# First two node tiles of the first linear share its weight rows, with matmuls on a tile of ones at the start

## What is computed

```
def sage(h, W_self, W_neigh, b):
    mean = segment_sum(h[src], dst) * deg_inv
    return h @ W_self + mean @ W_neigh + b
h   = relu(sage(x, W_self0, W_neigh0, b0))
x   = layernorm(x + sage(h, W_self1, W_neigh1, b1))
g   = x @ W.T + b                          # self loops added to the edges
out = layernorm(x + segment_sum(norm * g[col], row))
```

## Time and profile before

| | |
|---|---|
| median of 3 runs | 884.67 us (883.26 to 888.33) |
| span of the profiled execution | 879.3 us |
| time of that execution around its span | not given; the median lies 5.4 us above the span |
| mean granted TensorE clock | 0.995 |
| busy: TensorE, its weight loads, VectorE, ScalarE, GpSimd | 857.7, 731.8, 383.8, 142.9, 414.3 us |
| HBM | 114.83 MB read, 69.69 MB written |

### The profile page before, as it was taken

One profiled execution on the slowest core, in us unless ns is written; L12 is line 12 of the kernel. 1 busy time (PEld: TensorE's weight loads), 2 busy tenths in 40 slices (PEclk: granted clock), 3 DMA queues, 4 the chain that ended last, 5 costly groups with the idle time before them and its releaser, 6 DMA issues.

```text
span 879.3 us, 11251 instructions
## 1 busy us (share of the span) xinstructions
PE 857.7 (98%) x4403; PEld 731.8 (83%) x4403; DVE 383.8 (44%) x684; ACT 142.9 (16%) x199; POOL 414.3 (47%) x343
## 2 busy tenths in 40 slices
PE   6999999999899999999999999999999999999996
PEld 5888888888898899788888888888889889988885
DVE  5365669000037757411134112236664634555554
ACT  4111131202112113200031000011111212200000
POOL 2318878877878868877768857820000000000000
PEclk9999999999989999999999999999999999999999
DMA  8999665554777896433395788875648657755551
GB/s 305 312 425 349 213 195 144 142 153 110 183 234 214 263 291 197 116 100 98 102 360 175 241 269 286 249 221 165 215 132 291 206 167 249 252 187 196 194 192 47
DMA packets 111994, 185.56 MB, mean 211 GB/s; under 512 B 16526, under 2 KB 87190, under 8 KB 105792
## 3 DMA queue, kind: packets, MB, share of 16 engines
q1 hardware_dynamic: 60496, 113.56, 39.3%
q10 hardware_dynamic: 39056, 56.26, 18.1%
q0 software_dynamic: 12384, 14.95, 7.3%
HBM read 114.83 MB, written 69.69 MB: 210 GB/s over the span
## 4 chain that ended last, share of the span: by engine, by line
PE 90%; DVE 3%; DMA 3%; ACT 2%; issue 1%; ACTq 1%; SPq 0%; DVEq 0%
PE ps L1164 47%; PE ps L1192 11%; PE ps L1243 10%; PE ps L1257 10%; PE ps L1223 7%; DMA xin<-s0t_scr 2%; PE ps L1148 1%; PE ps L1106 1%; ACT outb L648 1%; PE ps L1116 1%; PE ps L1212 1%; DMA xin<-in_x 0%; ACT w L606 0%; DMA raw<-in_L_gnn_W_neigh 0%; DVE sacc L1039 0%
## 5 line engine op out<-in xcount | busy, mean ns | idle before, releaser
L1164 PE MATMUL ps<-w,xs 128*128 128x512 f32 x1440 | 335.0, 393 | 3.1 <-ACT w L606 1.8
L1164 PEld LDWEIGHTS ps<-w,xs 128*128 128x128 f32 x1440 | 270.2, 189 | 60.3 <-ACT w L606 3.0
L541 POOL DMA_INDIRECT adj_in<-mult,idx_in x160 | 199.9, 1250 | 82.2 <-issue 82.2
L541 POOL DMA_INDIRECT adj_out<-loops,idx_out x160 | 198.8, 1242 | 70.4 <-issue 66.0
L1192 PE MATMUL ps<-xs,w 128*128 128x512 f32 (+1 forms) x576 | 109.4, 351 | 1.2 <-ACT outb L648 1.1
L1192 PEld LDWEIGHTS ps<-xs,w 128*128 128x128 f32 x576 | 93.9, 189 | 16.8 <-ACT outb L648 1.8
L1164 PE MATMUL ps<-u,xs 128*128 128x512 f32 x432 | 98.2, 389 | 0.0
L1223 PE MATMUL ps<-w,u 128*128 128x256 f32 (+5 forms) x640 | 96.1, 312 | 0.0
L1164 PEld LDWEIGHTS ps<-u,xs 128*128 128x128 f32 x432 | 81.0, 188 | 16.8
L1223 PEld LDWEIGHTS ps<-w,u 128*128 128x128 f32 (+1 forms) x640 | 88.2, 194 | 6.6
L1243 PE MATMUL ps<-u,xs 128*128 128x512 f32 (+1 forms) x400 | 91.3, 390 | 0.3 <-issue 0.3
(11 more groups left out here) (135 smaller groups left out, 601.8 us busy)
## 6 DMA issues: line engine op xcount, KB each, us to landing
xs<-xt_scr SPq DMA_DIRECT2D x30, 1024.0 KB
xt_scr<-xs ACTq DMA_DIRECT2D x10, 1024.0 KB, 8.3
xin<-in_x SPq DMA_DIRECT2D x18, 512.0 KB, 7.4
xs<-xt_scr SPq DMA_DIRECT2D x16, 512.0 KB, 3.9
adj_in<-u POOLq DMA_DIRECT2D x4, 1600.0 KB, 26.1
adj_out<-u POOLq DMA_DIRECT2D x4, 1600.0 KB, 46.4
w<-adj_in SPq DMA_DIRECT2D x5, 1280.0 KB, 8.6
xs<-adj_in SPq DMA_DIRECT2D x10, 640.0 KB, 5.4
```

What stands on the lines that cost most here:

```text
L541: pool.indirect_dma_start(table, bass.IndirectOffsetOnAxis(ap=index[0:EP, j:j + 1], axis=0), counts[0:EP, j:j + 1], None, bounds_check=CEL ...
L1164: ins = nc.tensor.matmul(acc[:, cols], xs[:, t % 2, k, left * T:(left + 1) * T], w_row(q, k, right)[:, cols], start=(i == 0), stop=(i == l ...
```

## The change

It does five things.

- SyncE loads node tile 1 right after weight row 0.
- TensorE first runs 30 matmuls of 128 columns of a tile of ones with itself, into bank 7, as soon as VectorE's early memsets are done (`WARM_UP`).
- A new function `first_two` takes the place of `linear(N0, 0)` and `linear(N0, 1)`. For rows 0 to 4 (`SHARED = 5`) it does the steps of both tiles with a row before it goes to the next one; then tile 0 does rows 5 to 7 alone, and then tile 1. Tile 1 is turned right after the first pair of matmuls, into banks 6 and 7 (`turn_pair`), tile 2 between tile 0's last step and tile 1's own rows.
- ScalarE rounds tile 1 right after row 0's high part, stores turned tile 0 after row 5 and turned tile 1 after row 7. VectorE makes tile 1's low part right after row 0's.
- b0's transposition moves behind tile 1.

```diff
+    SHARED, WARM_UP = 5, 30
...
+        def turn_pair(t):
+            return 3 if t == 1 else 2
...
             load_x(0)
-            for k in range(4):
-                load_w(N0, k)
+            load_w(N0, 0)
             load_x(1)
-            for k in range(4, KD):
-                sp.wait_ge(w_lo_done, k - 3)
+            for k in range(1, KD):
+                if k >= 4:
+                    sp.wait_ge(w_lo_done, k - 3)
                 load_w(N0, k)
...
             for k in range(KD):
                 split_hi(N0, k)
-            store_turned(0)
-            for t in range(NT):
+                if k == 0:
+                    turn_hi(1)
+                elif k in (5, 7):
+                    store_turned(k // 2 - 2)
+            evict_hi(N0, 0)
+            for t in range(1, NT):
...
             for k in range(KD):
                 split_lo(N0, k)
+                if k == 0:
+                    turn_lo(1)
...
-                if t >= 1:
+                if t >= 2:
                     pe.wait_ge(xt_lo_done, t)
...
+            def first_two():
+                shared = []
+                for k in range(SHARED):
+                    for t in range(2):
+                        shared += [(t, k, 0, 0), (t, k, 1, 0)]
+                    if k >= 1:
+                        shared += [(0, k - 1, 0, 1), (1, k - 1, 0, 1)]
+                own = [[(t, SHARED - 1, 0, 1)] + [(t, k, left, right) for k in range(SHARED, KD) for left, right in ((0, 0), (1, 0), (0, 1))]
+                       for t in range(2)]
+                for i, (t, k, left, right) in enumerate(shared + own[0] + own[1]):
+                    if i == 1:
+                        turn_tile(1)
+                    elif i == len(shared) + len(own[0]):
+                        turn_tile(2)
+                    if k == 0:
+                        pe.wait_ge(xt_lo_done if left else xt_hi_done, t + 1)
+                    if t == 0 and left == 0:
+                        pe.wait_ge(w_lo_done if right else w_hi_done, k + 1)
...
+            pe.wait_ge(ones_ready, 3)
+            for _ in range(WARM_UP):
+                nc.tensor.matmul(ps[:, 7, 0:P], ones_r[:, :], ones_r[:, :], start=True, stop=True)
             pe.wait_ge(ident_ready, 1)
             turn_tile(0)
-            for t in range(NT):
-                linear(N0, t)
+            first_two()
+            for t in range(1, NT):
+                if t > 1:
+                    linear(N0, t)
```

More of the change, by code:

```diff
@@ L577, in turn_hi @@
                 act.wait_ge(xt_turned, t + 1)
+                if t == 1:
+                    act.wait_ge(xt_hi_done, 1)
                 if t >= 2:
                     act.wait_ge(xt_stored[t % 2], 16 * (t // 2))
-                nc.scalar.activation(xs[:, t % 2, :, 0:T], by_tile(pair_bank(2)), ACT.Copy).then_inc(xt_hi_done, 1)
+                nc.scalar.activation(xs[:, t % 2, :, 0:T], by_tile(pair_bank(turn_pair(t))), ACT.Copy).then_inc(xt_hi_done, 1)
             def store_turned(t):
@@ L772, in turn_lo @@
                 dve.wait_ge(xt_hi_done, t + 1)
-                nc.vector.tensor_tensor(xs[:, t % 2, :, T:2 * T], by_tile(pair_bank(2)), xs[:, t % 2, :, 0:T].bitcast(F32), ALU.subtract
+                nc.vector.tensor_tensor(xs[:, t % 2, :, T:2 * T], by_tile(pair_bank(turn_pair(t))), xs[:, t % 2, :, 0:T].bitcast(F32), ALU.subtract
                                         ).then_inc(xt_lo_done, 1)
@@ L906, in _ @@
                 if t + 1 < NT:
-                    turn_lo(t + 1)
+                    if t >= 1:
+                        turn_lo(t + 1)
                     if t == 1:
@@ L1102, in turn_tile @@
                 pe.wait_ge(x_full[t % 2], 16 * (t // 2 + 1))
-                if t >= 1:
+                if t >= 2:
                     pe.wait_ge(xt_lo_done, t)
                 for k in range(KD):
-                    ins = nc.tensor.transpose(ps[:, 4 + k // 4, k % 4 * T:(k % 4 + 1) * T], xin[:, t % 2, k * P:(k + 1) * P], ident[:, :])
+                    ins = nc.tensor.transpose(pair_bank(turn_pair(t))[:, k * T:(k + 1) * T], xin[:, t % 2, k * P:(k + 1) * P], ident[:, :])
                 ins.then_inc(xt_turned, 1)
@@ L1141, in linear @@
                 steps = sum((high[k] + (low[k - lag] if k >= lag else []) for k in range(KD)), []) + sum(low[KD - lag:], [])
-                if q == N0 and t == 0:
-                    steps[1:3] = steps[2:0:-1]
                 if q == GCN and t == NT - 1:
@@ L1152, in linear @@
                 for i, (k, left, right) in enumerate(steps):
-                    if q == N0 and t < NT - 1 and i == (16 if t == 0 else 4):
+                    if q == N0 and t < NT - 1 and i == 4:
                         turn_tile(t + 1)
@@ L1169, in linear @@
                         ins.then_inc(w_used, 1)
+            def first_two():
[16 more added lines that the diff above has]
+                        pe.wait_ge(w_lo_done if right else w_hi_done, k + 1)
+                    for n in range(2):
+                        cols = slice(n * BANK, (n + 1) * BANK)
+                        ins = nc.tensor.matmul(pair_bank(acc_pair(N0, t))[:, cols], xs[:, t, k, left * T:(left + 1) * T], w_row(N0, k, right)[:, cols],
+                                               start=(k + left + right == 0), stop=(k == KD - 1 and right == 1))
+                    if k == KD - 1 and right == 1:
+                        ins.then_inc(acc_full, 1)
             def self_turned():
@@ L1289, in _ @@
                     general = pe.value_load(flag[0:1, 0:1], min_val=0, max_val=1)
-                if t == 0:
-                    pe.wait_ge(ones_ready, 3)
+                if t == 1:
                     pe.wait_ge(b0_full, 16)
```

## The result

The changed kernel took 891.49 us (median of 6 runs, 888.39 to 894.06), the kernel before beside it 885.98 us (6 runs, 883.26 to 888.33): ratio 1.0067, 95% interval 1.0045 to 1.009. That is 5.5 us slower, outside the forecast range, which ended at 887.0 us.

A forecast was written before the change was run, and what follows sets the result against it. TensorE, busy 98% of the 879.3 us span, was taken as the bound; tile 1 ending 2.0 us early, less 1.2 us of new wait for the flag step, gained 0.8 us: 883.9 us, range 881.0 to 887.0.

The forecast's parts named there:

- the clock that was to be up before the linear: TensorE's clock was to rise at 6.3 to 7.1 us, so the first linear would start at the high level.
- the way of the edge lists to VectorE: Edge loads were to be released 1.35 us later with the same times to landing, the flag step done at 43.03 us.
- the mis-sized warm-up: 30 TensorE matmuls at 0.11 us each, done at 4.7 us, ahead of tile 0's landing at 5.19, costing nothing.
- the upper of my bounds: At most 0.213 us per 128-column warm-up matmul, with two passes; the warm-up would then end at 7.8 us.
- The 226-column row: Nearest profiled matmul form, 18 in 2.17 us, read as no more than one pass; used to take 0.11 us.
- rival 3: Warm-up on TensorE is in the way: tile 0 turned 1.4 us later, 885.3 us in total; chance 0.11.
- Rival 1: TensorE's clock doesn't come up before the linear: 885.0 us, or 886.1 if gaps delay the rise; chance 0.23.
- 2.2 us of slack: At TensorE's one-column flag-summing matmul in tile 2: VectorE's flag step ended at 41.68 us, the matmul ran at 43.89.
- my sum (33.7 + 8.14): Tile 1's end plus the way to the flag matmul: TensorE there at 41.85 us, waiting until about 43.05; 0.8 us gained.
- Later than 22.6 us the kernel is slower: Break-even for the end of row 7's high split on ScalarE, which gates the edge loads; forecast at 21.8 us.
- the absence of gaps behind the last of tile 1's row-0 pairs: From 12.25 us TensorE was to starve for nothing in the first linear, so tile 1 ends at 33.7 us.
- Rival 3's large case: Each short warm-up matmul costs as much as a 512-column one, 0.427 us: everything behind 7.9 us late, 891.7 us; chance 0.04.

The follow-up runs named there:

- e4: Changed kernel with 7 warm-up matmuls of 512 columns instead of 30 of 128; ratio 1.0035 to the kernel before.
- e2: Changed kernel with 14 warm-up matmuls of 128 columns instead of 30; ratio 1.0027 to the kernel before.
- e3: Kernel before with the 30 warm-up matmuls of 128 columns as its only change; ratio 1.0027 to the kernel before.
- e9: Changed kernel run once more, unaltered; ratio 1.0058 to the kernel before.
- e6: Changed kernel with 7 warm-up matmuls of 512 columns and edge loads issued behind row 4's high split instead of row 7's; ratio 0.9991 to the kernel before.
- e8: Kernel before with 7 warm-up matmuls of 512 columns and edge loads issued behind row 4's high split instead of row 7's; ratio 0.9993.
- e10: Changed kernel with 7 512-column warm-ups, edge loads behind row 4's high split, zero fills held until the edge lists landed; ratio 1.0031 to the kernel before.
- e14: Changed kernel with 7 warm-up matmuls of 512 columns and the flag matmul moved from tile 2 to tile 3; ratio 1.0007 to the kernel before.
- e1: Changed kernel without the warm-up matmuls, all else of the change kept; ratio 1.0052 to the kernel before.
- e16: Changed kernel without warm-up, stores of turned tiles 0 and 1 moved later on ScalarE; ratio 1.0023 to the kernel before.
- e11: Changed kernel without warm-up, zero fills held until the edge lists landed; ratio 1.006 to the kernel before.
- e13: Changed kernel without warm-up, flag matmul moved from tile 2 to tile 3; ratio 1.003 to the kernel before.

## Why the prediction was wrong

Two steps failed: the clock that was to be up before the linear, and the way of the edge lists to VectorE, which was to stay as long as it was. The first, with the mis-sized warm-up, made TensorE late; the second made the kernel slower even where the clock was up (e4).

- **Warm-up, mis-sized.** I took 0.11 us for a 128-column matmul of float32r; it took 0.213 from start to start, the upper of my bounds. The 226-column row that I let decide was of matmuls at the high clock, where a second pass or a fixed cost can't be read off a comparison with 512 columns at the low one. The first pair came 2.6 us later; rival 3 had 1.4 us for this, since it kept the transposes fast.
- **The clock, the first step that failed.** I had it up at 6.3 to 7.1 us. No narrow warm-up (changed, e2, e3, e9) raised it ahead of the linear; 7 wide matmuls, 3.36 us in all (e4, e6, e8, e10, e14), raised it before the linear's first pair in each profile. What part the transposes between play isn't separated by any run. Rival 1 happened, on top of rival 3. I had priced them apart, never together: with both, tile 1's rounding ends at 15.2 us instead of 10.96.
- **The way of the lists, the second step that failed.** I saw that row 7's high split gates the edge loads and that the flag matmul had 2.2 us of slack. I moved the gate by 1.35 us; it moved 5.7 in the changed kernel, 3.1 in e1 (24.30 against 21.16; rival 1 had 2.5) and 1.2 in e4, where the clock was up. From issue to key step I kept 17.3 us; it took 18.5 in the changed kernel, 19.3 in e1 and 20.5 in e4. So even with the forecast clock the flag matmul goes at 46.02 us (e4), not at 43.05, and with rival 1's clock the flag step is done at 46.8 (e1), not at 44.2. I had read this time from one profile; over the profiles it spreads by more than the slack.
- **Two terms that were missing.** A long wait at the flag matmul also costs the clock behind it: in six of the seven waits of 2.05 us and more the 24 matmuls behind took 7.1 to 7.9 us instead of 5.74. The restart at 243 us in the profile before showed just this, and I read it only for the time of a rise, not as the price of a new wait. And b0's transpose, moved behind tile 1, is in neither part of my sum (33.7 + 8.14); the second part takes 8.6 us with it.
- **Direction of the loss, right.** "Later than 22.6 us the kernel is slower" for row 7's split holds for e1 (23.55 us) and the changed kernel (26.1), but e4 is slower with a split that ended at 21.6. The order of work, the absence of gaps behind the last of tile 1's row-0 pairs, and the scatters moving with the rest (68.97 against 63.06) came as forecast.
- **A near hit that is luck.** Rival 3's large case says 891.7 us and the measured time is 891.49. It had 0.427 us for each short matmul; they took 0.213, and the time came about in another way.
- **The sum.** For the changed kernel: TensorE reaches the flag matmul 4.8 us later (2.6 of warm-up, 1.7 of the later rise and what goes with it, 0.5 behind tile 1), the lists are ready at the same moment, and 4.7 of 5.5 us stand at T9. Undoing only the warm-up frees TensorE and leaves the lists (e1, 4.6); undoing only the order leaves the warm-up (e3, 2.4). The two losses run side by side, so they don't add up.

The page "TensorE: Matmul & The Clock Gate" of the Trainium skill, section "Wait — 56ns, not 53.3ns?", gives 106.7 ns from start to start for 128 columns at the low clock; the trace shows 213 for this float32r form, twice that, and the measurement decides.

**Open:** why the edge lists take 17 to 26 us from issue to key step, and why issuing them 5.2 us earlier brings 1.1. Stretches of e1 while they are under way (length, then each engine's busy time, clock, DMA share, GB/s), and the DMA queues in the same two stretches (packets, MB, share of the engines):

```profile
24.00:30.00 6.00, 6.00 (x31) 4.98 (x30) 0.81 (x1) 0.29 (x1) 5.71 (x6) 1.00 1.00 397
30.00:36.00 6.00, 6.00 (x30) 4.77 (x28) 2.36 (x2) 2.51 (x3) 2.52 (x5) 1.00 0.84 178
```

```profile
q10 hardware_dynamic: 256, 1.86, 75.1%
q1 hardware_dynamic: 127, 0.44, 18.1%
q0 software_dynamic: 217, 0.07, 6.2%
```

```profile
q0 software_dynamic: 430, 0.97, 78.6%
```

Queue q0 carries what GpSimd issues, the lists and the fills. The bytes of q10 fit the two 1 MB stores of turned tiles, issued at 18.28 and 22.50 us. Up to 30 us that queue has 75.1% of the engines' time and the lists' 6.2%; then q0 has most of it, at less than half the bytes per us of the first stretch. In e6, whose lists are issued at 15.96 us, q0 moves one packet up to 22 us, while q1, the loads, has 87.1%. So the lists get little of the engines at first. But e16, with later stores, gained no more than the spread, and e11 waits for the lists with half-idle engines, so sharing the engines is not all of it. No run issues the lists from another engine or in larger pieces; that rival is untested. The spread of the clock's rise is unexplained too: 2.9 to 9.4 us after the linear's first matmul in the kernels without a wide warm-up, and 9.4 both with 30 narrow matmuls ahead (changed) and with none (e13).

No version here beats the kernel before by more than the measurement can tell: the best is e6, 0.9991 (0.9974 to 1.0008).

## What to carry to other kernels

Before an engine's work is brought forward, find what its next cross-engine wait has as slack, and follow that slack's chain back through every queue the change pushes: here 2.2 us of slack stood behind a gate that moved 1.2 to 5.7 us, and behind a transfer whose length differed by more than the slack from profile to profile. Price a new wait on TensorE as its length plus slow matmuls behind it (1.4 to 2.1 us after six of the seven waits of 2.05 to 4.76 us here). Of the two widths tried for a warm-up only the wide one worked, and even it brought no time that the runs can tell from none. Look at start-to-start times to see whether it worked, since the clock column reads 1.00 from the beginning.

## What the runs showed of the hardware that I had not expected

- A 128x128 float32r matmul costs 0.213 us at the low clock, half of a 512-column one (0.427), not a quarter, and as much as a 256-column one at that clock in the kernel before (the 26 of the earlier trace rows, 0.213 from start to start).
- 30 such matmuls, 6.66 us without a gap, raised no clock ahead of the linear (changed, e3, e9); 7 of 512 columns, 3.36 us, did (e4, e6, e8, e10, e14).
- Waits of 2.05, 3.15, 3.51, 4.16, 4.46 and 4.76 us at the flag matmul were each followed by a stretch at the granted clock 0.50; waits of 0.76 and 0.93 us were not, and one of 2.90 us (e10) wasn't either.
- Edge-list loads issued at 15.7 us landed for the key step at 41.8 us (e10), while those issued at 24.0 were there at 40.9 (e13).
